# A softmax step with six gathers on GpSimd, and the same step with two of them made by SyncE transfers

## The reference, cut to what matters

```python
_, lut = jax.lax.top_k(blk_scores, T)                 # T = 6 of 64 blocks
kg = jnp.take_along_axis(kr[:, :, None], idx, axis=3) # their keys
vg = jnp.take_along_axis(vr[:, :, None], idx, axis=3) # their values
p = jax.nn.softmax(jnp.einsum('bhnqd,bhnkd->bhnqk', qr, kg) * scale, axis=-1)
o_s = jnp.einsum('bhnqk,bhnkd->bhnqd', p, vg)
```

## Time and profile before

| | us |
|---|---|
| median of 3 runs | 9206.59 |
| lowest, highest run | 9197.57, 9220.26 |
| the profiled execution: its time | 9182.84 |
| the profiled execution: its span | 9181.0 |
| busy in the span: PE, DVE, ACT, POOL | 7700.7, 5035.6, 3517.2, 3781.4 |
| granted TensorE clock, mean | 0.917 of full speed |

### The profile page before, as it was taken

How to read it: one execution, slowest core, us unless ns; L and a number is a source line. 1 busy time by engine, 2 the same in 40 slices (tenths; PEclk the granted TensorE clock), 3 DMA queues, 4 the chain that set the end, 5 groups by cost and what they waited for, 6 DMA issues and landing times.

```text
span 9181.0 us, 193051 instructions
## 1 busy us (share of the span) xinstructions
PE 7700.7 (84%) x58476; PEld 5340.1 (58%) x58476; DVE 5035.6 (55%) x11563; ACT 3517.2 (38%) x9207; POOL 3781.4 (41%) x10084
## 2 busy tenths in 40 slices
PE   8978799788997889978799788997889978799777
PEld 6645566555665556655566555665556655566555
DVE  3475644756447564475644656447564465644656
ACT  1144621455214552144521445214552145521455
POOL 2335533355333553344533355333553345533454
PEclk9988899888998889988899888998889988999889
DMA  3201122011220112201122011220112201122011
GB/s 99 64 15 26 38 88 64 15 26 38 88 64 15 26 38 87 64 15 27 41 84 64 15 26 38 88 64 15 27 42 83 64 15 27 46 78 64 18 25 54
DMA packets 398691, 431.05 MB, mean 47 GB/s; under 512 B 159184, under 2 KB 355984, under 8 KB 393296
## 3 DMA queue, kind: packets, MB, share of 16 engines
q1 hardware_dynamic: 397648, 418.42, 16.1%
HBM read 102.76 MB, written 67.63 MB: 19 GB/s over the span
## 4 chain that ended last, share of the span: by engine, by line
PE 54%; DVE 23%; issue 7%; DMA 6%; ACT 5%; DVEq 3%; SPq 1%; POOL 1%; POOLq 0%; ACTq 0%
PE PS L621 12%; PE PS L681 7%; DVE arena L1129 5%; PE PS L899 5%; DVE arena L1216 4%; PE PS L768 4%; PE PS L638 3%; PE PS L661 3%; PE PS L864 3%; PE PS L824 3%; PE PS L833 3%; DVE SM L1340 3%; DMA kv_rows<-arena 3%; ACT arena L1073 2%; DVEq L1328 2%
## 5 line engine op out<-in xcount | busy, mean ns | idle before, releaser
L968 ACT ACTIVATE arena<-PS 128x128 f32<-128x128 f32 (+5 forms) x4160 | 1549.5, 398 | 2080.8 <-PE PS L621 595.3
L559 POOL COPY arena<-arena 64x129 f32 x6144 | 1528.8, 291 | 1400.3 <-PE PS L870 1130.3
L483 POOL TENSOR_TENSOR arena<-arena 128x512 f32<-128x512 f32 x768 | 803.9, 1069 | 1493.1 <-PE PS L621 1477.7
L621 PE MATMUL PS<-arena 128*128 128x256 f32 x6144 | 1359.1, 379 | 48.1 <-DMA arena<-arena 43.1
L1129 DVE COPY arena<-PS 64x260 f32<-64x260 f32 (+2 forms) x1272 | 634.1, 514 | 1373.8 <-PE PS L621 527.9
L621 PEld LDWEIGHTS PS<-arena 128*128 128x128 f32 x6144 | 1157.7, 189 | 270.5 <-issue 96.2
L1129 DVE COPY arena<-arena 64x129 f32 x4096 | 845.9, 268 | 409.8 <-PE PS L870 292.5
L804 PE MATMUL PS<-arena 64*64 64x192 f32 x8192 | 710.6, 390 | 252.0 <-POOL arena L559 225.2
L1216 DVE RECIPROCAL arena<-arena 128x512 f32<-128x512 f32 x256 | 857.6, 3350 | 115.6 <-ACT arena L1016 114.1
L489 POOL TENSOR_TENSOR BUF<-BUF,arena 128x512 f32<-128x512 f32 x256 | 358.1, 1399 | 1287.1 <-ACT arena L1004 1287.1
L1340 DVE TENSOR_REDUCE SM<-PS 128x1 f32<-128x384 f32 x1024 | 570.8, 557 | 549.9 <-issue 419.5
(11 more groups left out here) (102 smaller groups left out, 11208.6 us busy)
## 6 DMA issues: line engine op xcount, KB each, us to landing
arena<-arena SPq DMA_DIRECT2D x1024, 128.0 KB, 2.3
arena<-arena SPq DMA_DIRECT2D x768, 144.5 KB
BUF<-in_x SPq DMA_DIRECT2D x18, 2048.0 KB, 11.7
kv_rows<-arena SPq DMA_DIRECT2D x256, 130.0 KB, 3.5
arena<-kv_rows SPq DMA_DIRECT2D x256, 130.0 KB
out<-BUF SPq DMA_DIRECT2D x64, 512.0 KB, 2.6
arena<-in_taps SPq DMA_DIRECT2D x96, 288.0 KB, 3.7
W<-in_w SPq DMA_DIRECT2D x2, 768.0 KB, 5.9
```

Of the source, the lines that this page charges most:

```text
L483: last = pool.tensor_tensor(o, tap, mix, ALU.mult)
L559: last = pool.tensor_copy(G[p % GD][0:D, j // 3, j % 3, :], KVB[0:D, bass.ds(off, KVW)])
L621: last = nc.tensor.matmul(bank(i)[:, a * 256:(a + 1) * 256], lhsT=TW[n % 2][:, a * CH + k * P:a * CH + (k + 1) * P], rhs=src[:, k // 2:k / ...
L968: return nc.scalar.activation(o, i, ACT.Copy)
```

## The change

For each step, the third of GpSimd's three rows of each query block (index 2 of the lower half) is no longer copied by GpSimd. SyncE reads the two offsets into two registers of its own, waits until the buffer is free (s_o, as GpSimd did), and issues two transfers from SBUF to SBUF, 64 partitions x 129 floats each. `scores(p)` waits for their landing as well, on one of four new semaphores. GpSimd loads four offsets and makes four copies a step. The issues of `q_to_upper(2)` to `(7)` go into the new loop, behind the transfers of p = 5, 9, 13, 17, 21 and 25. The loop begins after `kv_in(7)`.

```diff
+            sp_regs = [sp.alloc_register(f"offset{k}") for k in range(2)]
...
                         kv_in(6)
                         kv_in(7)
-                        for q in range(2, QUADS):
-                            q_to_upper(q)
-
+                        sp.wait_ge(s_kv2, (hd + 1) * TP)
+                        sp.wait_ge(s_ir[hl], (b * 2 + h // 2 + 1) * 16)
+                        settle(sp)
+                        for p in range(NP):
+                            sp.load(sp_regs, pair_offsets(hl, p)[:, :, 2:3])
+                            if p >= GD:
+                                sp.wait_ge(s_o, hd * NP + (p - GD + 1))
+                                settle(sp)
+                            for blk in range(2):
+                                off = sp.snap(sp_regs[blk], min_val=0, max_val=LAST)
+                                sp.dma_start(G[p % GD][0:D, blk, 2, :], KVB[0:D, bass.ds(off, KVW)]
+                                             ).then_inc(s_gs[p % GD], 16)
+                            if p % 4 == 1 and 5 <= p < NP - 4:
+                                q_to_upper((p + 3) // 4)
...
-            pool_regs = [pool.alloc_register(f"offset{j}") for j in range(6)]
+            pool_regs = [pool.alloc_register(f"offset{j}") for j in range(4)]
...
-                                pool.load(pool_regs, pair_offsets(hl, p)[:, :, 0:3])
+                                pool.load(pool_regs, pair_offsets(hl, p)[:, :, 0:2])
...
-                                for j in range(6):
+                                for j in range(4):
                                     off = pool.snap(pool_regs[j], min_val=0, max_val=LAST)
-                                    last = pool.tensor_copy(G[p % GD][0:D, j // 3, j % 3, :],
+                                    last = pool.tensor_copy(G[p % GD][0:D, j // 2, j % 2, :],
                                                             KVB[0:D, bass.ds(off, KVW)])
...
                                 for s in (s_gp, s_ga, s_gd):
                                     pe.wait_ge(s, hd * NP + p + 1)
+                                pe.wait_ge(s_gs[p % GD], (hd * (NP // GD) + p // GD + 1) * 32)
```

More of the change, by code:

```diff
@@ L281, in build @@
         s_gp = sem("gathered_by_pool")
+        s_gs = [sem(f"gathered_by_transfer{i}") for i in range(GD)]
         s_ga = sem("gathered_by_act")
```

## The result

The changed kernel took 9785.35 us (median of 4 runs, 9766.19 to 9813.51) against 9204.66 us for the kernel before (4 runs, 9197.57 to 9220.26): 1.0639 times as long, interval 1.0602 to 1.0676. The prediction said 9297 us and a range up to 9440. The sign was right, the size six times too small, and the time lies outside the range. The profiled spans are 9181.0 us before and 9764.4 us after, so 583 us are to be found.

A forecast was written before the change was run, and what follows sets the result against it. VectorE's chain was taken to bound the kernel, with GpSimd's queue nearly full. Steady steps, +26 us, and starts of heads, +64 us, made +90 us on 9206.6: 9297 us, range 9165 to 9440.

The forecast's parts named there:

- What bounds the kernel now: Steady steps of 2.49 us: VectorE's chain is the longer path, GpSimd's queue nearly full at 2.2 to 2.3 us.
- GpSimd's side: Gathers in the steps: GpSimd's queue falls to about 1.2 us a step, giving at most 60 or 95 us.
- rival 1: Faster, 9170 us: SyncE's loop hides, GpSimd's relief shows, VectorE's copies may shorten up to 0.1 us a step; chance 0.18.
- SyncE's throughput: SyncE's queue in a step: 2.0 us, or 2.5 us with a q_to_upper, fitting in the step of 2.49.
- The latency, 2.96 us: In a step, from the end of apply(p-4) through two issues and a 1.9 us landing to scores, against GpSimd's 1.87.
- +26 us in the sum: Steady steps: the loop through SyncE makes the mean step 2.52 us against 2.49, over 864 steps.
- scores to the end of apply, 2.0 us: TensorE's part of the two-step loop: about 0.6 us for scores and 1.41 us for turn and apply.
- The start of a head, +64: SyncE reaches its loop only after kv_in(7), so complements begins 2.0 us later in each head, +64 us.
- rival 3: Clearly slower, 9448 us (+241): transfers land at 2.3 us or later, sharing transfer engines with q_to_upper and kv_in; chance 0.20.
- A landing of 2.3 us would prove it wrong: Test on the changed profile: landings expected at 1.8 to 2.0 us; 2.3 us would prove the sum wrong.
- The steady step: Steady steps in the changed profile: about 2.5 us each; under 2.45 us would prove the sum wrong.

The follow-up runs named there:

- the late load: The kernel before with VectorE's load of its offsets moved from ahead of the maxima to behind them; 9078.21 us, 0.9863.
- the full loop beside the work: The kernel before with all six copies, plus SyncE's loads and two transfers a step into three spare buffers nobody reads; 9195.95 us, 1.0016.
- the small filler: The changed kernel with one 128x64 matmul a step whose result nobody reads, 10487.06 us, 1.1437; on the combined version with one transfer, 10417.68 us, 1.1362.
- the filler: The changed kernel with one more 128x256 matmul a step behind apply(p-2), its result never read; 9692.30 us, 1.0561.
- the order of the waits: The changed kernel with the wait of scores for the transfers moved behind its other waits, ahead of settle; 9688.26 us, 1.0572.
- the run that takes it back: The changed kernel with steps 0 to 3 of each head gathered by GpSimd alone, transfers from step 4 on; 9664.51 us, 1.0531.

## Why the prediction was wrong

- **What bounds the kernel now:** right. VectorE's chain set the pace (the late load, 1.4% faster) and GpSimd's queue was nearly full behind it (747 waits once VectorE was out of the way).
- **GpSimd's side:** its copies fell by 493 us (1528.8 to 1035.5), forecast some 510. What that was to give, up to 60 or 95 us, never came: four copies alone, with other data, made the kernel 1.8% slower. VectorE's copies, which rival 1 had up to 0.1 us a step shorter, took 282 ns each instead of 268. In the sum the relief stood as nothing, and it may have been a loss of up to 0.9%. Rival 1 falls with it.
- **SyncE's throughput:** right. Issue 0.50 us, load 0.47 us, and the full loop beside the work cost 0.2%. The prediction's estimate of 2.08 us for a landing, by the Trainium skill (DMA: Bandwidth & Descriptors, section Anatomy of one DMA), goes by a figure for transfers issued by GpSimd; SyncE's landed in 1.8 us in the median.
- **The latency, 2.96 us:** the parts to the landing were 0.18 + 0.64 + 1.8 = 2.62 us against a predicted 2.82, so better in the common case. But a mean was needed and a typical value was put in: with the tail the mean is 2.97 us to the landing. The wake of TensorE was 0.35 us and not 0.14; two instructions of 0.106 us, the wait for the exponentials and `settle`, ran in it. From `scores` to the end of `apply` were 2.10 us in the mean and not 2.0. The loop is 2.97 + 0.35 + 2.10 = 5.42 us instead of 4.96, 2.71 us a step at full clock. The line's 76.0 us for 28 steps are 2.71 as well. This term, +26 us in the sum, measured 180 to 210 us: its mechanism was right, its size was not.
- **The clock, the step that failed most:** "scores to the end of apply, 2.0 us" and every duration of TensorE were taken from rows at full clock, as if a longer loop left them alone. The loop through SyncE is longer than the work in it, TensorE idles, the share at 1.2 GHz goes from 0.144 to 0.496, and there the scores take 0.92 us instead of 0.56, and from `scores` to the end of `apply` are 3.22 us instead of the 2.0 of the prediction. That is some 260 us that stand in no term. What makes the clock fall isn't shown. More idle time went with a larger share in the changed kernel, but other data alone raised the share too, and the small filler held the low level without any idle time. That the clock costs time the filler shows from one side (clock back, 0.8% faster with more work), the order of the waits from another (one wait instruction less behind the transfer, 0.7% less time, three quarters of the steady part's gain by the clock). The Trainium skill (TensorE: Matmul & The Clock Gate, section HAM oscillation — how this bites in real kernels) tells of matmuls in short bursts with waits of 3 to 5 us for a transfer between them, where the clock falls again and again. This trace shows the same with shorter waits: the longest idle time of TensorE in a steady part is 2.5 us (before 1.7), and the share is 0.496 against 0.144.
- **The start of a head, +64:** right in kind. `complements` began 6.5 us after the last issue of `kv_in(7)`, before 4.1: +2.4 x 32 = 77 us, its wait for kv_rows gone; with what follows 105 us, and 99 by the run that takes it back.
- **Rivals:** rival 3 (9448, +241) had the right direction for the wrong reason: the median landing stayed 1.8, and what stood beside every late one was an instruction packet, not `q_to_upper`. "A landing of 2.3 us would prove it wrong" tested the median, which was blind to both causes. The steady step, forecast at about 2.5 us, came to 3.1 in the mean (87.3 us for 28).

The sum as it should have been: 210 + 260 + 105 = 575 us, and with the 8 us ahead of the first head the 583.

Open: why other data, and perhaps fewer copies on GpSimd, lower TensorE's clock, why the 64-column filler holds it at 1.2 GHz, and whether without instruction packets the two transfers would fit; a kernel without them wasn't tried.

## What to carry to other kernels

A transfer inside a loop that frees and refills buffers is priced at its mean landing with its tail, not at its median, and the time that it adds can cost as much again by TensorE's clock: read the granted clock of the stretch and price the loop at both levels. Put the wait that comes last at the end of the waits. Before an engine is relieved, look which chain is in front of it: here another order of two calls on VectorE gave 1.4%, where two transfers for GpSimd cost 6.4%.

## What the runs showed of the hardware

- A filler of 128x64 on TensorE in each step held it at 1.2 GHz for the whole steady part in two kernels (steady 107.3 us a head); one of 128x256 lifted the share at 2.4 GHz from 0.50 to 0.85, two of them to 1.00. The Trainium skill (TensorE: Matmul & The Clock Gate, section What's actually happening) has it that activity releases the throttle. The runs with 256 columns agree. With 64 columns TensorE was busy for 107.28 of 107.30 us by the profile and stayed at 1.2 GHz, which differs, and the runs decide.
- Instruction packets share the DMA engines with the kernel's transfers: 1068 in the profiled execution, and every one of the 253 landings over 2.05 us, of a transfer that else takes 1.8, had one beside it.
- The same instructions on other data: 0.9% slower, with a share at 1.2 GHz of 0.268 instead of 0.144. A third of GpSimd's copies less, again on other data: 1.8% slower, share 0.353.
- At 1.2 GHz a step of this kernel is 3.2 us of TensorE's work without a gap; at 2.4 GHz the same work is done in 2.65 us with waits.
